# Inputs laid out for the layers, a front without turns, and the next tile's first layer ahead of this tile's second

## The reference

```
L0  a = layernorm(cond)*g + b;  h = gelu(a @ w1 + b1);  xw = h @ w2 + b2      # w2: [512, 8192]
    x_a, x_b = halves of xw, each reshaped to [b, 512, rank 8]
    layer[b] = base + x_a[b] @ x_b[b].T;  x = x + (x + x @ layer[b])           # so x0 = 2x + x @ layer
L1  x = x + tanh(x @ W_ih.T + cond @ W_hh.T + b_hh + b_ih)
L2  LSTM over the 2048 steps: gates = x_t @ Wx + h @ Wh + b (2048 gates);  x = x + h
L3  the same with other weights, on L2's output
```

## Time and profile before

| | us |
|---|---|
| median of three runs | 11880.57 |
| the profiled execution | 11879.89 |
| its span on the core | 11878.0 |
| TensorE (PE) busy | 11821.8 |
| VectorE (DVE) busy | 8287.9 |
| ScalarE (ACT) busy | 3254.8 |
| GpSimd (POOL) busy | 1422.2 |

### The profile page before, as it was taken

One profiled execution on the slowest core, in us unless ns is written; L12 is line 12 of the kernel. 1 busy time (PEld: TensorE's weight loads), 2 busy tenths in 40 slices (PEclk: granted clock), 3 DMA queues, 4 the chain that ended last, 5 costly groups with the idle time before them and its releaser, 6 DMA issues.

```text
span 11878.0 us, 432877 instructions
## 1 busy us (share of the span) xinstructions
PE 11821.8 (100%) x232412; PEld 2720.0 (23%) x100764; DVE 8287.9 (70%) x46342; ACT 3254.8 (27%) x20602; POOL 1422.2 (12%) x5238
## 2 busy tenths in 40 slices
PE   8999999999999999999999999999999999999999
PEld 5222222222222222222222222222222222222222
DVE  2677777777777777777777777777777777777776
ACT  2222222222222222222222222222222222222222
POOL 4011111111111111111111111111111111111110
PEclk9999999999999999999999999999999999999999
DMA  4000000000000000000000000000000000000000
GB/s 165 25 4 5 4 5 4 5 5 4 5 5 4 5 5 4 4 5 5 4 5 5 4 5 5 4 5 5 5 4 5 5 4 5 5 4 5 5 5 4
DMA packets 374516, 107.65 MB, mean 9 GB/s; under 512 B 349594, under 2 KB 357830, under 8 KB 372436
## 3 DMA queue, kind: packets, MB, share of 16 engines
q1 hardware_dynamic: 362372, 61.96, 2.8%
q0 software_dynamic: 3504, 11.56, 0.3%
q10 hardware_dynamic: 6560, 6.32, 0.2%
HBM read 62.98 MB, written 16.78 MB: 7 GB/s over the span
## 4 chain that ended last, share of the span: by engine, by line
PE 99%; DVE 0%; issue 0%; ACT 0%; POOL 0%; POOLq 0%
PE bank L80 89%; PE bank L888 7%; PE bank L518 1%; PE bank L531 1%; PE bank L898 0%; PE bank L484 0%; DVE gates_t L1080 0%; DVE wx L544 0%; DVE gates_t L1091 0%; DVE turned L1048 0%; DVE state L1117 0%; DVE state L1114 0%; ACT gate_o L970 0%; DVE state L1110 0%; DVE pre L1086 0%
## 5 line engine op out<-in xcount | busy, mean ns | idle before, releaser
L80 PE MATMUL bank<-wh,state 128*6 128x512 bf16 x197472 | 11056.3, 378 | 8.1 <-DVE state L1117 8.1
L1079 DVE STREAM_TRANSPOSE gates_t<-bank 128x256 f32<-128x256 f32 x4096 | 1844.0, 450 | 2199.2 <-PE bank L80 2197.7
L80 PEld LDWEIGHTS bank<-wh,state 128*6 128x6 bf16 x65824 | 1590.9, 86 | 7374.6 <-issue 6491.0
L965 ACT ACTIVATE gate_if<-pre 128x16 f32<-128x16 f32 x4096 | 899.1, 220 | 7258.1 <-DVE pre L1084 7258.1
L1110 DVE TENSOR_TENSOR state<-gate_o,tanh_c 128x8 f32<-128x8 f32 x4096 | 688.8, 168 | 851.9 <-ACT tanh_c L972 817.0
L1091 DVE STREAM_TRANSPOSE gates_t<-bank 128x128 f32<-128x128 f32 x4096 | 1253.1, 306 | 0.0
L1080 DVE STREAM_TRANSPOSE gates_t<-bank 128x128 f32<-128x128 f32 x4096 | 1123.1, 274 | 0.0
L970 ACT ACTIVATE gate_o<-pre 128x8 f32<-128x8 f32 x4096 | 861.6, 210 | 950.1 <-DVE pre L1097 950.1
L1003 POOL TENSOR_TENSOR y<-x,state 128x8 f32<-128x8 f32 x2048 | 435.3, 213 | 5349.1 <-DVE state L1117 5349.0
L1003 POOL TENSOR_TENSOR x<-x1r,state 128x8 f32<-128x8 f32 x2048 | 435.6, 213 | 4958.9 <-DVE state L1117 4958.9
L972 ACT ACTIVATE tanh_c<-g_c 128x8 f32<-128x8 f32 x4096 | 859.9, 210 | 10.8 <-DVE g_c L1101 10.8
(11 more groups left out here) (123 smaller groups left out, 2952.9 us busy)
## 6 DMA issues: line engine op xcount, KB each, us to landing
w<-in_w SPq DMA_DIRECT2D x8, 2048.0 KB, 13.5
out<-y_rows SPq DMA_DIRECT2D x1020, 8.0 KB, 1.8
wx<-in_x SPq DMA_DIRECT2D x16, 512.0 KB, 5.2
x1p<-x_t_all SPq DMA_DIRECT2D x128, 64.0 KB, 2.7
x1r<-x_t_all SPq DMA_DIRECT2D x128, 64.0 KB, 2.6
x_t_all<-wx ACTq DMA_DIRECT2D x6, 1024.0 KB, 4.8
wx<-in_Wh POOLq DMA_DIRECT2D x8, 512.0 KB, 4.1
wx<-in_Wh POOLq DMA_DIRECT2D x16, 256.0 KB, 4.6
```

Of the source, the lines that this page charges most:

```text
L80: return pe.add_instruction(mybir.InstMatmult(name=nc.get_next_instruction_name(), engine=mybir.EngineType.PE, ins=[pe.lower_ap(moving), p ...
L965: act.activation(gate_if[l][:, :, :, 1], pre[l][:, 0:2 * HB].rearrange("p (w n) -> p w n", w=2), ACT.Sigmoid).then_inc(S[l]["if"], 1)
L1079: dve.transpose(gates_t[l][:, 0:gf, NS * NB:], banked[:, 0:gf]).then_inc(s["trans_if"], 1)
```

## The change

The host now hands the inputs over in other layouts (`laid_out`): x as [128, block, batch, time], W_ih and W_hh transposed, w2 and b2 with the rank outside the feature within each piece of 1024. The copies to rank order and every turn go. w2 gets four buffers, which the products read directly; SP asks for a piece again when its product is done. W_hh goes straight to `whh_t` on GpSimd's queue. W_ih goes straight to `wih_t`, but on SP's queue, behind w2 and tile 0. SP issues tiles 0 to 3 before the barrier.

A tile of x is now loaded into one of the four blocks of `wx3` (`HOME`), summed there in place, and stored from there. Tiles 4, 6 and 5 are loaded when the second, second and third store has landed, tile 7 after the fifth. In the front the first layer has one set of banks and the second the other, and TensorE does tile u's first layer before tile u - 1's second. Tile 5's second layer comes after the first projections. VectorE waits for all four blocks of a first layer before it sums them, does the memset and the turned quarters between the sums of tile 4, and has two waits for stores in chunk 0.

The core of the diff:

```diff
-    NW2 = 3
+    NW2 = 4
-        def put_by_rank(copy, eng, k, half):
...
-            copy(ranked[:, hs, :, :], w2[k % NW2][:, hs, :].rearrange("p h (d r) -> p h r d", r=RANK)
-                 ).then_inc(s_ranked[half], 1)
...
                     if k >= NW2:
-                        for half in range(2):
-                            sp.wait_ge(s_ranked[half], k - NW2 + 1)
-                    load_blocked(sp, w2[k % NW2][:, :, :], ins["w2"][:, W2N * n:W2N * n + W2N], s_w2[k % NW2])
-                    if k == 1:
-                        turn.load_rows(sp, 0)
-                sp.wait_ge(turn.s_turn, NH)
-                turn.load_rows(sp, 1)
+                        sp.wait_ge(s_xw, k - NW2 + 1)
+                    load_blocked(sp, w2[k % NW2][:, :, :, :].rearrange("p h r d -> p h (r d)"),
+                                 ins["w2"][:, W2N * n:W2N * n + W2N], s_w2[k % NW2])
+                turn.load(sp, 0)
+                load_blocked(sp, wih_t[:, :, :], ins["W_ih"], keep["s_wih"])
+                for u in range(1, 4):
+                    turn.load(sp, u)
...
-                pool.dma_start(whh[:, :, :], ins["W_hh"].rearrange("(a p) i -> p a i", p=P)).then_inc(s_whh, DMA)
+                load_blocked(pool, whh_t[:, :, :], ins["W_hh"], s_whh)
...
-                pool.dma_start(wih[:, :, :], ins["W_ih"].rearrange("(a p) i -> p a i", p=P)).then_inc(s_wih, DMA)
...
                 def product(k):
-                    for half in range(2):
-                        pe.wait_ge(s_ranked[half], k + 1)
+                    pe.wait_ge(s_w2[k % NW2], (k // NW2 + 1) * DMA)
...
                 product(0)
+                product(1)
+                product(2)
                 pe.wait_ge(s_whh, DMA)
-                for k in range(4):
-                    turned(whh, k)
-                product(1)
-                pe.wait_ge(s_wih, DMA)
-                for k in range(4):
-                    pe.wait_ge(s_whh_t, k + 1)
-                    turned(wih, k)
-                product(2)
                 rows_by_tile(by_row[:, P:2 * P], cond_p, whh_t).then_inc(s_term_r, 1)
...
-                pe.wait_ge(s_wih_t, 4)
-                turn.transpose(pe, 0, bank)
...
+class Tiles:
+    HOME = (3, 2, 1, 0, 2, 1, 3, 2)
...
+    def load(self, eng, u):
+        eng.dma_start(self.of(u).rearrange("p h (b t) -> p h b t", b=NB),
+                      self.ins["x"][:, :, :, TILE * u:TILE * u + TILE]).then_inc(self.s_x[u % 4], DMA)
+    def loaded(self, eng, u):
+        eng.wait_ge(self.s_x[u % 4], (u // 4 + 1) * DMA)
...
     def x0_of(self, u):
-        return self.turn.of(u + len(self.turn.x_t) - 1)
+        return self.turn.of(u) if u < NFRONT else self.turn.area[(0, 3)[u - NFRONT]]
...
@@ SP @@
-                for u in range(2, NFRONT + 1):
-                    sp.wait_ge(turn.s_turn, NH * u)
-                    turn.load_rows(sp, u)
+                for u, stored in ((4, 2), (6, 2), (5, 3)):
+                    sp.wait_ge(tiles.s_store, stored * DMA)
+                    turn.load(sp, u)
                 sp.wait_ge(*cut_done)
                 load_gate_blocked(sp, wx[L2][:, :, :], ins["Wx2"], s_wx2)
...
-                sp.wait_ge(turn.s_turn, NH * (NFRONT + 1))
-                turn.load_rows(sp, NFRONT + 1)
+                sp.wait_ge(tiles.s_store, 5 * DMA)
+                turn.load(sp, 7)
@@ TensorE @@
-                        if u + 1 < NTILE:
-                            pe.wait_ge(turn.s_copy, NH * (u + 1) + ho)
-                            turn.turn_block(pe, u + 1, ho, spare)
...
-                for u in range(NFRONT):
-                    for ho in range(NH):
-                        tiles.first(pe, u, ho, banks(u, 0)[ho])
-                    for h in range(NH):
-                        if u:
-                            pe.wait_ge(tiles.s_x1, NH * (u - 1) + h + 1)
-                        turn.turn_block(pe, u + 1, h, banks(u, 1)[h])
-                    for ho in range(NH):
-                        tiles.second(pe, u, ho, banks(u, 2)[ho])
-                pe.wait_ge(turn.s_copy, NH * (NFRONT + 1))
+                def first_of(u):
+                    for ho in range(NH):
+                        if u:
+                            pe.wait_ge(tiles.s_x0, NH * (u - 1) + ho + 1)
+                        tiles.first(pe, u, ho, sets[0][ho])
+                def second_of(u):
+                    for ho in range(NH):
+                        if u:
+                            pe.wait_ge(tiles.s_x1, NH * (u - 1) + ho + 1)
+                        tiles.second(pe, u, ho, sets[1][ho])
+                first_of(0)
+                for u in range(1, NFRONT):
+                    first_of(u)
+                    second_of(u - 1)
+                pe.wait_ge(tiles.s_x0, NH * NFRONT)
                 pe.wait_ge(s_wx2, NRUN * DMA)
                 for n in range(CH + AHEAD):
                     project(L2, Chunk(0, 0), n // CH, *divmod(n % CH, NH))
+                second_of(NFRONT - 1)
                 chunks(pe, emit)
@@ VectorE @@
+                def sums0(u):
+                    dve.wait_ge(tiles.s_l0, NH * u + NH)
                     for h in range(NH):
-                        tiles.sum0(dve, u, h, banks(u, 0)[h])
+                        tiles.sum0(dve, u, h, sets[0][h])
+                sums0(0)
+                for u in range(1, NFRONT):
+                    sums0(u)
+                    dve.wait_ge(tiles.s_l1, NH * u)
+                    if u == NFRONT - 1:
+                        dve.wait_ge(s_init, 12)
+                        dve.wait_ge(tiles.s_x0, NH * NFRONT)
+                        dve.memset(gates[L2][:, :], 0.0).then_inc(S[L2]["r2"], 1)
                     for h in range(NH):
-                        tiles.sum1(dve, u, h, banks(u, 2)[h], tiles.x0_of(u))
+                        tiles.sum1(dve, u - 1, h, sets[1][h], tiles.x0_of(u - 1))
+                        if u == NFRONT - 1:
+                            turn_quarter(L2, Chunk(0, 0), 0, h)
+                dve.wait_ge(tiles.s_l1, NH * NFRONT)
+                for h in range(NH):
+                    tiles.sum1(dve, NFRONT - 1, h, sets[1][h], tiles.x0_of(NFRONT - 1))
                 chunks(dve, emit)
...
+def laid_out(short, a):
+    if short == "x":
+        return a.reshape(NB, T, NH, P).transpose(3, 2, 0, 1)
+    if short in ("W_ih", "W_hh"):
+        return a.T
+    if short in ("w2", "b2"):
+        by_rank = a.reshape(a.shape[:-1] + (NH * 2, P, RANK))
+        return by_rank.swapaxes(-1, -2).reshape(a.shape)
+    return a
```

More of the change, by code:

```diff
@@ L178, in condition @@
         s_w1, s_b1 = m.sem("c_w1"), m.sem("c_b1")
-        s_whh, s_wih = m.sem("c_whh"), m.sem("c_wih")
+        s_whh = m.sem("c_whh")
         s_bias = m.sem("c_bias")
@@ L183, in condition @@
         s_b2 = m.sem("c_b2")
-        s_ranked = [m.sem(f"c_ranked{i}") for i in range(2)]
         s_zero, s_ident, s_select = m.sem("c_zero"), m.sem("c_ident"), m.sem("c_select")
@@ L362, in _ @@
                                    bias=b1_t[:, h:h + 1]).then_inc(s_gelu, 1)
-                put_by_rank(act.copy, act, 0, 0)
-                for k in range(4):
-                    act.wait_ge(s_turn, k + 1)
-                    act.copy(whh_t[:, k, :], bank[k][:, :]).then_inc(s_whh_t, 1)
-                put_by_rank(act.copy, act, 1, 0)
-                for k in range(4):
-                    act.wait_ge(s_turn, 4 + k + 1)
-                    act.copy(wih_t[:, k, :], bank[k][:, :]).then_inc(s_wih_t, 1)
-                put_by_rank(act.copy, act, 2, 0)
-                put_by_rank(act.copy, act, 3, 0)
-                turn.copy(act, 0, bank)
-                for k in range(HALF, NPIECE):
-                    put_by_rank(act.copy, act, k, 0)
             @block.tensor
             def _(pe):
-                def turned(rows, k):
-                    for a in range(4):
-                        mm = pe.transpose(bank[k][:, P * a:P * a + P], block_cols(rows[:, a, :], k), ident[:, :])
-                    mm.then_inc(s_turn, 1)
                 def rows_by_tile(out, columns, moving):
@@ L527, in second @@
     def second(self, pe, u, ho, to):
+        if u == 0 and ho == 0:
+            pe.wait_ge(self.s_wih, DMA)
         if ho == 0:
@@ L809, in last_tiles @@
                     store_x1(NFRONT)
+                    load_wx3(0)
+                    sp.wait_ge(tiles.s_store, (NFRONT + 1) * DMA)
                     load_wx3(1)
-                    sp.wait_ge(tiles.s_store, (NFRONT + 1) * DMA)
-                    load_wx3(0)
                     sp.wait_ge(tiles.s_x0, NH * NTILE)
@@ L976, in emit @@
                                     tiles.tanh(act, u, h, sets[1][h])
-                                elif u + 1 < NTILE:
-                                    act.wait_ge(tiles.s_store, u * DMA)
-                                    turn.copy_block(act, u + 1, h, spare)
                 for u in range(NFRONT):
+                    for h in range(NH):
+                        tiles.tanh(act, u, h, sets[1][h])
```

(12 more changed lines are left out.)

73 lines of the change are left out of this document (14 added, 59 removed).

## The result

The kernel after took 11847.93 us, the median of nine runs (11846.65 to 11849.62), against 11881.51 us for the kernel before in the same comparison (11879.41 to 11883.04). The ratio is 0.9971, 95% interval [0.9963, 0.9979]; the medians lie 33.6 us apart, where 33.5 had been forecast.

A forecast was written before the change was run, and what follows sets the result against it. TensorE was taken to bound the kernel, with only work ahead of 403 us able to move: 20.8 + 10.5 - 0.9 + 1.3 + 1.8 = 33.5 us off 11879.89, plus 0.7 to the median, made 11847, range 11838 to 11860.

The forecast's parts named there:

- Start of the front: End of the conditioning stage: without copies and early loads, TensorE starts the front at 62.3 instead of 83.1, gaining 20.8 us.
- Bytes: Conditioning stage: at 0.409 MB/us on the queues, the last w2 piece is there at 54.8 us.
- SP's issuing: Before the front's barrier: SP's last tile issue, held up by outstanding packets, puts the start between 61.3 and 62.9.
- third case: The first x1 load behind Wx2 in the kernel before: its issue ended with 2229 packets outstanding, against 1718 and 1676.
- Turns: Front: six tiles each lose a 1.75 us turn, 10.5 us gained, less 0.9 lost once at tile 1.
- New waits: Front: loads of tiles 4 and 5 wait for stores with 14 us slack, Wx2 has 18; no cost.
- Hand-over: From front to step 0: projections after tile 4 wait less for sums and turn, 1.3 us gained (bounds 0 and 1.5).
- Chunk 0: Four turned blocks of tile 7, 0.44 us each, go: 1.8 us gained; everything later, low clock included, left unchanged.
- Cold bursts (B): Conditioning stage: TensorE idles before each product and runs at the low clock, start 67.3, total 11852; chance 0.15.
- Slow tile loads (C): Before the front: tile loads in 1 KB runs move at half a store's rate, start 70, total 11855; chance 0.12.
- Wx2 in the turns' place (D): Before the projections: Wx2 still lands at 232, TensorE stands 17 us, total 11864; chance 0.10, lesser late loads included.
- A slower loop (E): Recurrence: some 2030 steps each grow; 17 ns a step eats the gain, 25 ns gives 11897; chance 0.05.

The follow-up runs named there:

- loads_early: The kernel after with tile 0 loaded behind w2's second piece and W_ih on GpSimd's queue, as the kernel before does; one execution, 11853.84 us.
- best: As `warm`, but SP issues tiles 2 and 3 behind the barrier instead of before it; 11844.59 us, ratio 0.9967 to the kernel before.
- old_order: The kernel after, sums still in place, but each tile's second layer right after its first, tile 5's ahead of the projections; 11868.49 us, ratio 0.9989.
- wx2_late: The kernel after with Wx2's load held back until the fourth store has landed; one execution, 11848.44 us.
- after_again: The kernel after, unchanged, timed and profiled a second time; 11848.49 us, ratio 0.997 to the kernel before.
- warm: The kernel after with unread matmuls filling TensorE's waits in steps 14 and 15, chunk 1's first steps and the tail; 11844.77 us, ratio 0.9967.
- copies_back: The kernel after with w2 again put in rank order by on-chip copies, and three w2 buffers; 11866.59 us, ratio 0.9986 to the kernel before.
- three_buffers: The kernel after with three buffers for w2 instead of four; one execution, 11848.57 us.
- before_warm: The kernel before with the same three places filled by matmuls as in `warm`; 11879.31 us, ratio 0.9997 to the kernel before.
- w2_alone: The kernel before with only w2 and b2 laid out by rank and read directly from four buffers, all turns kept; 11861.35 us, ratio 0.9983.
- copies_warm: As `copies_back`, plus three unread matmuls on TensorE ahead of each of the first five products; one execution, 11856.29 us.

## Why the prediction was right, and where it was not

**What bounds the kernel: right.** TensorE's queue is the path; only work ahead of 403 us moved, and the 11475 us behind it moved by 2.3.

**1. Start of the front: right in kind, 1.2 us too small.** Forecast was 62.3, measured 61.14. Bytes (54.8 against 54.84) and chain (5.9 plus 0.4 at the barrier) were as worked out, and `loads_early` shows that bytes do it. The mis-sized term is SP's issuing, which the forecast had set the start by: it took 1680 packets outstanding at the end of an issue, near two of its three cases. By 60.44 us SP's queue had moved 6922 packets of 9316:

```profile
q1 hardware_dynamic: 6922, 20.55, 88.0%
```

(packets, MB, share of the 16 engines, in the view of the DMA queues of the kernel after up to 60.44.) That is 2394 outstanding, the like of the third case (2229), which had given 61.0 for SP's end and 61.3 for the start. That the tile loads would move at a store's 347 GB/s was right: 365 GB/s in 54:61 and 349 in 61.1:66. With SP's end and VectorE's level, SP set the start by 0.4 us, as `best` shows, and not by 1.6.

**2. Turns: right** (10.5; tile 1 cost 1.05, not 0.9). The forecast had priced the missing cover at 2.8 us a tile; `old_order` measures 2.65, and shows what the forecast did not add up: sums in place without the new order lose what the turns gave and 7 us more, so the two halves of the edit need each other.

**3. New waits: right.** Wx2 was issued at 181.72 (forecast 181.6), and `wx2_late` shows at least 12 us of slack (forecast 18). Tiles 4 and 5 were never waited for.

**4. Hand-over: 1.5 instead of 1.3.** Projections 4.50 us; tile 5's second layer ran without a gap into step 0.

**5. Chunk 0: right in its 1.8; "whatever follows I leave as it is" was not.** The blocks at 336 and 343 and the tail's ran at the low clock in the profiled execution and cost 3.2 us and 1.7; against the trace of before, which has one such block, that is a loss of 1.9 and 1.7, and the back edges take 1.1 more. Every run of `after_again` lay 1.6 to 5.2 us above the median of `warm` beside it, so by this estimate each of them had such losses, the back edges' included. That the difference of medians came out at the forecast 33.6 is in part luck: 1.4 us too little for start and hand-over together stand against a loss that was not foreseen; with the places filled the two kernels are 34.5 apart. The profiled pair alone, from which the forecast was worked out, gave 30.2; the forecast's 0.7 us from profiled execution to median was -1.7 in the kernel after.

**The rivals.** Cold bursts (B): one product, at 29.17, with no effect. Behind it the products waited 1.82 us at most, the last three 0.15 to 0.32, and ran short; the mechanism is real, and cost `copies_back` 8.6 us. Slow tile loads (C): refuted by the 349 to 365 GB/s. Wx2 in the turns' place (D): refuted by its issue at 181.72 and by `wx2_late`. A slower loop (E): 2.3 us in 11475, which is 1 ns a step and comes from the single places above.

**Open, and what the traces say of it.** All thirteen traces hold the loop's two back edges. The 90 us around each, measured between VectorE's transposes for the output (`y_rows`), take 90.3 to 90.9 and 90.5 to 90.6 us in seven of them (after twice, wx2_late, loads_early, three_buffers, copies_back, old_order) and 89.9 to 90.0 in the other six (before, before_warm, w2_alone, copies_warm, warm, best). The same seven, and no others, have the slow tail (4.35 to 4.47 us against 2.79). It is not the clock that costs the time at the back edges: it was 1.00 in 4150:4250 of after. TensorE stands idle for nothing that the profile shows ("issue") in the midst of a block of matmuls:

```profile
4208.55 1.67 PE L80 MATMUL bank<-wh,state 128*6 128x512 bf16 x27 [0.31 <-issue]
```

Such an idle stretch, of 0.17 to 0.58 us, stands near at least one back edge in each of the seven traces and near none in the six. After's two executions agree, and `copies_warm` leaves the seven by a few matmuls added 4000 us earlier, which speaks for the program and against chance in the execution. That the place of TensorE's instructions in memory decides it would fit, but is not shown. A third place is like them: the 90 us near 11410 us of before, where by the 3596 us from one stall to the next the loop ends, take 89.8 or 89.9 in w2_alone, copies_back and copies_warm, 90.9 to 91.1 in eight others, before and after among them, and 92.0 in `warm` and `best`. There TensorE waits for a turn on VectorE, 0.88 us in before and 1.02 in after, and in `warm` it also idles 0.86 us for nothing that the profile shows. This place is what `warm` loses and most of what w2_alone gains in the loop.

## What to carry to other kernels

Where a stage waits for copies, the price of a copy is its own time and what the wait does to the clock of the matmuls behind it; here the second (8.6 us) was almost as large as the first (10.6), and no row of copy durations shows it. A difference of 1 to 3 us in 11850 can come from places that the edit never touched: compare the unchanged stretches of several traces before giving such a difference to the edit. When copies go, ask which bytes stand ahead of the last one needed, and put the other loads behind them: that order alone was 5.6 us. An in-place sum takes away a turn but ties the next layer to the sum, so it pays only with other work between the two.

## What the runs showed of the hardware

- Counting a packet per row or run, issues on SP's queue ended when between 1640 and 2510 packets were outstanding: 1643 behind W_ih's rows of 2 KB, 1779 behind w2's, and 2156, 2514, 2380 and 2394 behind the four tiles in runs of 1 KB. One issue took up to 9.99 us.
- After the same idle time the same matmuls ran at either level of the clock. Of twenty blocks of 48 after 2.07 to 2.16 us of idling in ten traces, thirteen took 4.17 to 4.45 us and seven 2.76. Of ten tails of 96 after 2.37 us, seven took 4.35 to 4.47 us and three 2.79. After 0.64 us of idling, with filler before it, all took 2.76 or 2.79.
- A layer of 64 or 32 matmuls that starts after a wait mostly takes 0.24 to 0.27 us more than one that follows at once (14.07 and 14.08 against 13.81, 13.97 against 13.73). The wait alone does not explain it: tile 5's second layer took 13.93 right behind the projections.
- Loads in runs of 1 KB at a pitch of 64 KB moved at 349 GB/s, 13% below the 401 of w2's rows (45:54).
